# Negated row maxima as three rows of the stacked query operand, placed by a DMA for each batch, in a six-stage decoder kernel

## The reference

```python
q = (x @ wq + bq) / sqrt(8); k = c @ wk + bk; v = c @ wv + bv     # c is x, or the context (64, 77, 128)
attn = softmax(einsum('bhqd,bhkd->bhqk', q, k), axis=-1)
out = einsum('bhqk,bhkd->bhqd', attn, v)
x = layernorm(x + (out @ wo + bo))
```

## Time and profile before

| | us |
|---|---|
| Median of 3 runs | 5520.02 (5518.24 to 5530.13) |
| The profiled execution | 5516.31 |
| Its span in the trace | 5514.6 |
| First scores to the tail of F / N / Y in the trace | 3240 to 3750 / 4204 to 4755 / 4820 to 5258 |
| PE busy in the span | 4032.9 (73%) |
| DVE busy | 4394.4 (80%) |
| ACT busy | 2740.3 (50%) |
| POOL busy | 3137.7 (57%) |

### The profile page before, as it was taken

One profiled execution on the slowest core, in us unless ns is written; L12 is line 12 of the kernel. 1 busy time (PEld: TensorE's weight loads), 2 busy tenths in 40 slices (PEclk: granted clock), 3 DMA queues, 4 the chain that ended last, 5 costly groups with the idle time before them and its releaser, 6 DMA issues. The chain is left out here.

```text
span 5514.6 us, 104615 instructions
## 1 busy us (share of the span) xinstructions
PE 4032.9 (73%) x29692; PEld 2318.9 (42%) x29692; DVE 4394.4 (80%) x8517; ACT 2740.3 (50%) x6405; POOL 3137.7 (57%) x3426
## 2 busy tenths in 40 slices
PE   5777787777777877775788958885465888698843
PEld 2333233333323333232466636664464666466611
DVE  5999999999999999997688867764245777676678
ACT  3545554554555545553577724444564555344434
POOL 6877777777777777785677732324553222333302
PEclk8999899998998989988899969996786888799955
DMA  2111111111011101110566446654125555365511
GB/s 83 66 43 58 68 67 48 54 67 68 33 68 67 67 37 65 68 66 13 92 113 106 80 90 111 110 102 146 53 86 99 93 103 100 74 115 107 99 39 31
DMA packets 320201, 420.84 MB, mean 76 GB/s; under 512 B 40000, under 2 KB 301713, under 8 KB 309137
## 3 DMA queue, kind: packets, MB, share of 16 engines
q1 hardware_dynamic: 315536, 408.35, 31.9%
q0 software_dynamic: 4352, 8.95, 0.5%
HBM read 307.65 MB, written 109.58 MB: 76 GB/s over the span
## 5 line engine op out<-in xcount | busy, mean ns | idle before, releaser
L2199 POOL TENSOR_TENSOR m_h<-m_dtu,m_Bb 128x512 f32<-128x512 f32 x1024 | 1589.8, 1581 | 225.8 <-PE bank L1834 218.9
L1834 PE MATMUL bank<-m_h,ident 128*128 128x512 f32 x2048 | 1215.6, 684 | 497.3 <-DVE m_h L2098 484.3
L1834 PEld LDWEIGHTS bank<-m_h,ident 128*128 128x128 f32 x2048 | 361.6, 206 | 1162.5 <-DVE m_h L2098 1016.6
L2092 DVE TENSOR_TENSOR_SCAN m_h<-m_dA,m_h 128x512 f32<-128x512 f32 x512 | 755.2, 1475 | 6.3 <-DVE m_sz L2025 6.3
L2098 DVE TENSOR_TENSOR m_h<-m_h,bank 128x512 f32<-128x512 f32 x1024 | 672.3, 657 | 5.3 <-DVE m_h L2092 2.9
L2092 DVE TENSOR_TENSOR_SCAN m_h<-bank,m_h 128x512 f32<-128x512 f32 x512 | 620.5, 1212 | 28.1 <-DVE m_sz L2025 11.8
L1981 ACT ACTIVATE bank<-m_dt,m_A 128x512 f32<-128x512 f32 x512 | 352.4, 688 | 494.7 <-DVE m_h L2092 436.1
L1981 ACT ACTIVATE m_dA<-m_dt,m_A 128x512 f32<-128x512 f32 x512 | 367.2, 717 | 430.6 <-DVE m_h L2092 426.8
L688 DVE TENSOR_REDUCE x_nm<-bank 128x4 f32<-128x308 f32 x512 | 242.8, 474 | 182.3 <-PE bank L359 179.2
L531 ACT ACTIVATE x_sm<-bank,x_nm 128x77 f32<-128x77 f32 x1024 | 317.9, 335 | 59.9 <-DVE x_nm L688 59.4
L688 DVE TENSOR_REDUCE f_nm<-bank 128x4 f32<-128x512 f32 x256 | 175.8, 688 | 119.2 <-PE bank L359 118.6
(11 more groups left out here) (425 smaller groups left out, 10400.9 us busy)
## 6 DMA issues: line engine op xcount, KB each, us to landing
m_Bb<-m_B SPq DMA_DIRECT2D x32, 4096.0 KB, 12.1
x_Ks<-x_k_parts SPq DMA_DIRECT2D x32, 462.0 KB
x_q_parts<-x_qp SPq DMA_DIRECT2D x32, 384.0 KB, 4.1
x_Qs<-x_q_parts SPq DMA_DIRECT2D x32, 384.0 KB
f_Ks<-f_k_parts SPq DMA_DIRECT2D x16, 768.0 KB
a_Ks<-a_k_parts SPq DMA_DIRECT2D x16, 768.0 KB
x_xp<-x_stage SPq DMA_DIRECT2D x32, 256.0 KB
x_Qs<-x_q_parts SPq DMA_DIRECT2D x32, 256.0 KB
```

The costliest lines, as they stand in the source:

```text
L1834: pe.matmul(banks[4 + c], ident[:], h[:, k % RING, :], start=(s == 0), stop=(s == NS - 1)).then_inc(s_ya.sem, 1)
L2092: v.tensor_tensor_scan(h[:, k % RING, :], decays[k % AHEAD], h[:, k % RING, :], 0.0, ALU.mult, ALU.add).then_inc(s_h.sem, 1)
L2199: pool.tensor_tensor(h[:, k % RING, :], dtu[:, d, c, :], Bb[:, d, s, :], ALU.mult).then_inc(s_dB.sem, 1)
```

## The change

In stages without a gate the negated maxima no longer have matmuls of their own. They are three more rows of `Qs`, rows 96 to 98, against rows of ones in `Ks`. The scores are taken with these rows at zero, `shifted` with the maxima in them:

- ACT issues one DMA for each batch (`place_rows`), from `nmT` (48 rows x 128) to three rows x 16 heads x 128 of `Qs`, as soon as `nmT` is there. `sel`, its three selections on POOL and its matmuls are gone.
- `fill_stack` sets the three rows of a group back to zero by one more DMA, from rows 99 to 101.
- `shifted` and `exp` of a batch begin two slots later: chunk 0 in slot 3 of the next step, and chunks 1 to 3 in slots 0 to 2 of the step after that. `values` stays in its slots. The wait for `nmT` in `shifted` becomes a wait for the DMA.
- The stacks' rows are 0 to 23 and 64 to 87 (in stage X too). The 48 rows of `Ks` come in two DMAs of 24, and the memset of `Ks` in two, rows 0 to 95 and 96 to 127, the latter 1.0 without a gate and 0.0 with one.

```diff
-    PARTS, ROWS = 3, 6 * DH
+    PARTS = 3
     K_TIMES = (3, 2, 1)
+    Q_ROWS = (0, 8 * DH, 10 * DH)
+    K_ROWS = ((0, 0, 3), (8 * DH, 3, 6))
+    MAX_ROW = 96
+    FILLS = len(Q_ROWS) + len(K_ROWS) + (gate is None)
+    T_AT = 3
...
+        def turned_chunk(c):
+            return (1, c - T_AT) if c >= T_AT else (2, c - T_AT + 4)
+        def placed(i, lb):
+            return s_mr[lb % 2].sem, s_mr[lb % 2].at(4 * (i + lb // 8) + lb % 8 // 2 + 1)
...
-                at = 0
-                for parts in K_TIMES:
-                    fill(Qs[at * DH:(at + parts) * DH, par], dram_q[par, 0:parts])
-                    at += parts
-                fill(Ks[0:ROWS, par], dram_k[par])
+                for row, parts in zip(Q_ROWS, K_TIMES):
+                    fill(Qs[row:row + parts * DH, par], dram_q[par, 0:parts])
+                if gate is None:
+                    sp.dma_start(Qs[MAX_ROW:MAX_ROW + PARTS, par], Qs[MAX_ROW + PARTS:MAX_ROW + 2 * PARTS, par]).then_inc(s_stk[par].sem, 16)
+                for row, lo, hi in K_ROWS:
+                    fill(Ks[row:row + (hi - lo) * DH, par], dram_k[par, lo:hi])
...
-            def shifted(b, lb, c):
+            def shifted(b, lb, c, rows):
                 l, q = lb // GB, lb % GB
-                pe.wait_ge(s_nmT.sem, s_nmT.at(b + 1))
+                pe.wait_ge(*rows)
                 pe.wait_ge(s_e.sem, s_e.at(b, c + 1 - 2))
                 for h in range(4):
                     hh = 4 * c + h
                     o = bankT[c % 2][0:sk, h * S:(h + 1) * S]
-                    pe.matmul(o, Ks[:, l, hh, q * sk:(q + 1) * sk], Qs[:, l, hh, q * S:(q + 1) * S],
-                              start=True, stop=False)
-                    ins = pe.matmul(o, sel[:, hh, 0:sk], nmT[:, lb % 2, :], start=False, stop=True)
+                    ins = pe.matmul(o, Ks[:, l, hh, q * sk:(q + 1) * sk], Qs[:, l, hh, q * S:(q + 1) * S],
+                                    start=True, stop=True)
...
+            def place_rows(b, lm, rows):
+                act.wait_ge(s_nmT.sem, s_nmT.at(b + 1))
+                act.sem_inc(s_step, 1)
+                q = lm % GB
+                act.dma_start(Qs[MAX_ROW:MAX_ROW + PARTS, lm // GB, :, q * S:(q + 1) * S], nmT[0:PARTS * H, lm % 2, :]).then_inc(rows, 16)
...
-            dve.memset(Ks[:], 0.0).then_inc(s_zero.sem, 1)
-            if gate is None:
-                dve.memset(nmT[:], 0.0).then_inc(s_zero.sem, 1)
+            dve.memset(Ks[0:MAX_ROW], 0.0).then_inc(s_zero.sem, 1)
+            dve.memset(Ks[MAX_ROW:P], 1.0 if gate is None else 0.0).then_inc(s_zero.sem, 1)
```

More of the change, by code:

```diff
@@ L87, in attention @@
     TAIL = 6
-    ident, identb, ones_row, sel = const["ident"], const["identb"], const["ones_row"], const["sel"]
+    ident, identb = const["ident"], const["identb"]
     half_pow = const["half_pow"]
@@ L170, in attention @@
         s_mid = sem("mid_ready", 2); s_lo = sem("lo_ready", 2)
-        s_ps = sem("parts_stored", 16 * (PARTS + 1)); s_stk = [sem(f"stack_loaded{l}", 16 * (PARTS + 1)) for l in range(2)]
+        s_ps = sem("parts_stored", 16 * (PARTS + 1)); s_stk = [sem(f"stack_loaded{l}", 16 * FILLS) for l in range(2)]
         s_ln = sem("front_var", 1); s_lp = sem("front_pow", 1); s_xn = sem("front_norm", 1)
@@ L174, in attention @@
         s_S = sem("scores", 4); s_Sf = sem("scores_used", 4); s_nmp = sem("max_parts"); s_T = sem("max_transposed")
-        s_nmT = sem("max_rows"); s_st = sem("shifted", 4); s_e = sem("exp", 4)
+        s_nmT = sem("max_rows"); s_mr = [sem(f"max_rows_placed{p}", 16) for p in range(2)]; s_st = sem("shifted", 4); s_e = sem("exp", 4)
         s_gp = [sem(f"gate_loaded{l}", 16) for l in range(2)]; s_tw = sem("weights_turned", 4); s_ev = sem("weights_copied", 4)
@@ L187, in attention @@
         bankMb = bankM.bitcast(BF16)
-        NZ = 2 + (gate is None) + (sk < P)
+        NZ = 3 + (sk < P)
         NW = sum(1 for t in (bq, bk, bv, bo) if t is not None) + 4 + (2 if ln is not None else 0) + (2 if rms else 0)
@@ L431, in step @@
                         turn_weights(b - 1, (lb - 1) % 8, c)
[L432 to L435, removed]
+                else:
+                    k, chunk = turned_chunk(c)
+                    if live(k):
+                        shifted(b - k, (lb - k) % 8, chunk, placed(i, lb - k))
+                    if c == 0 and live(1):
                         turn_max(b - 1, (lb - 1) % 8)
-                elif live(1):
-                    shifted(b - 1, (lb - 1) % 8, c - 1)
                 if live(2):
@@ L546, in step @@
                 else:
[L547 to L550, removed]
+                    k, chunk = turned_chunk(c)
+                    if live(k):
+                        exp(b - k, (lb - k) % 8, chunk)
                 if c == 0 and live(4):
@@ L554, in step @@
                     act.activation(oT[:], bankY[:, 0:S], ACT.Copy).then_inc(s_oT.sem, 1)
+                if c == 0 and live(1) and gate is None:
+                    place_rows(b - 1, (lb - 1) % 8, placed(i, lb - 1)[0])
             def slots(i, lb, c, last):
@@ L699, in split_maxima, with maxima_rows @@
                 v.tensor_tensor(nmp[:, p, 2, :], nm[:, p, 1, :], nmp[:, p, 1, :], ALU.subtract).then_inc(s_nmp.sem, 1)
-            def maxima_rows(v, ch, b, lm):
+            def maxima_rows(v, ch, b, lm, rows):
                 v.wait_ge(s_T.sem, s_T.at(b + 1))
-                v.wait_ge(s_st.sem, s_st.at(b - 1))
+                v.wait_ge(*rows)
                 v.tensor_copy(nmT[0:PARTS * H, lm % 2, :], bankMb[0:PARTS * H, 0:S]).then_inc(s_nmT.sem, 1)
@@ L755, in step @@
                 if c == 0 and live(1) and gate is None:
-                    maxima_rows(v, ch, b - 1, (lb - 1) % 8)
+                    maxima_rows(v, ch, b - 1, (lb - 1) % 8, placed(i, lb - 3))
                 if gate is not None:
@@ L2628, in constants @@
     ones_row = st.enter_context(nc.sbuf_tensor("ones_row", [1, P], F32))
-    sel = st.enter_context(nc.sbuf_tensor("sel", [P, H, P], BF16))
     half_pow = st.enter_context(nc.sbuf_tensor("half_pow", [P, 4 * GB], F32))
@@ L2636, in _ @@
             pool.memset(identb[:], 0.0).then_inc(s, 1)
-            pool.memset(sel[:], 0.0).then_inc(s, 1)
             pool.memset(ones_row[:], 1.0).then_inc(s, 1)
             pool.memset(half_pow[:], -0.5).then_inc(s, 1)
-            pool.wait_ge(s, 5)
+            pool.wait_ge(s, 4)
             pool.affine_select(out=ident[:], in_=ident[:], compare_op=ALU.not_equal, fill=1.0, base=0,
@@ L2644, in _ @@
                                pattern=[[-1, P]], channel_multiplier=1).then_inc(s, 1)
[L2645 to L2650, removed]
+            pool.wait_ge(s, 6)
+    return {"ident": ident, "identb": identb, "ones_row": ones_row, "half_pow": half_pow}
 def build(nc, a, out, stages="MXFNYQ"):
```

## The result

The changed kernel takes 5779.4 us (median of 4 runs, 5775.3 to 5781.9) against 5519.4: a ratio of 1.047, 95% interval 1.0455 to 1.0485. It is slower, and 219 us above the top of the predicted range. Its profiled execution spans 5775.7 us, 261 more than before.

What follows compares the result with a forecast made beforehand. PE was nearest to full, F and Y mostly following it, N largely DVE; terms -115 + 15 + 19 + 4 + 25 - 8 + 10 + 1 + 6 = -43 gave 5477 us, forecast 5470, range 5385 to 5560.

Steps and rivals of the forecast that it cites:

- The new DMA: Placing the maxima in `Qs`: lands in 2.3 us, one 0.4 us stall a group, +19 us, bounds 0 and +130.
- In the long ones the slack is over 4 us: Time to spare for the placed rows in a group's long steps, against 1.9 to 2.2 us in its shortest.
- The matmuls removed: 1024 `sel` matmuls fewer on PE in each of F, N and Y: -115 us, bounds -50 and -165.
- The two slots: `shifted` two slots later leaves the exponential one slot ahead of `values`, sometimes late: +15 us, bounds 0 and +60.
- The fill: Stack loads, 17.6 us in F and 14.8 in Y: +4 us at four stage starts, +25 in mid-stage.
- A: Rival: everything hides, fill 12.2 us in F and never late, 5353 us, or 5400 with half; chance 0.22.
- B: Rival: the fill becomes the bound, 20 us in F, 17 in Y; 5574 at worst, some 5520; chance 0.15.
- Starts: Kernel start without `sel` setup -8 us; second memset +10 in N, +1 elsewhere; first and last steps +6.
- C: Rival: placed rows late in every step before `shifted` of chunk 0; slower, 5557 to 5717 us; chance 0.12.
- D: Rival: DVE takes over at once, -50 us in place of -115, 5505 to 5520 us; chance 0.11.
- 15 to 20% behind PE: DVE's busy time against PE's in stages F, N and Y, as read from the earlier profile.
- three steps less two slots of 1.3 and less 2.0: Time left for Y's mid-stage fill: 15 us before unevenness, about equal to the need of 14.8.

Runs made afterwards that it cites:

- e1: Changed kernel without the placement DMA, maxima left out of the exponent: 5392.5 us, ratio 0.975 to the kernel before.
- e2: Changed kernel with the stack filled only for the first two groups of each stage without a gate, placements kept: 5485.3 us, ratio 0.992.
- e10: Kernel before with only `shifted` and the exponential moved two slots later, one-hot matmuls and old rows kept: 5443.6 us, ratio 0.983.
- e11: Kernel before with only the new stack rows (0-23 and 64-87), five fills in place of four: 5513.5 us, ratio 0.997.
- e13: Kernel before without its one-hot matmuls (maxima left out of the exponent), old order kept: 5461.9 us, ratio 0.988.
- e16: Kernel before with the two-slot move and the new rows, one-hot matmuls kept, no placement DMA: 5399.1 us, ratio 0.977.

## Why the prediction was wrong, step by step

**The new DMA** is the step that failed. It said: "I take 2.3 us, from 1.6 to 5 when it shares the engines with a fill", and hence +19, bounds 0 and +130. The 2.3 was about right where no fill is under way (2.2 to 3.7 us where PE waited for it). The upper bound was the miss: beside a fill it took 11.1 to 14.5 us in F and N, 8.7 to 10.3 in Y. The term is +386 us (score sum of e1 to that of the changed kernel). I had taken the 5 us for a price of sharing bandwidth; it is a place in a line, so its bound was the fill's own length, and that stood in the earlier trace rows: 16.6 and 13.8. The earlier trace rows had the fill's issue (3503.12) 6 us ahead of the next turn of the maxima (3508.94), so that this placement had to fall inside the fill. The 391 us of waits are near the 386 in sum, but not by stage: 161, 115 and 115 of waits against 103, 124 and 159 of time. Of the 386, 290 go with the fills (e2); in the other 96 is the issue on ACT, for which I took SP's 0.33 us where it takes 0.74.

**"In the long ones the slack is over 4 us"** failed with it. The placement hit was that of the third step of a group, issued 4 us behind the fill. The short first step, which I watched, has none of more than 1 us in the groups that I read.

**The matmuls removed**: -115, bounds -50 and -165; measured -50 in the old order and -25 or -17 in the new. The sum priced PE's work where PE set the pace. In F it set it less than its 85% of busy time said, and PE's work there fell by 28 us less than the 62, at a lower clock.

**The two slots**: +15, bounds 0 and +60; measured -86. The sign is wrong. I asked who comes closer together (exponential and `values`: e10 has 9.8 us of such waits in N) and not who comes apart (`nmT` and `shifted`). By luck the two errors nearly cancel: matmuls, move and rows give -126, where my terms for matmuls and move gave -100.

**The fill**: +4 at the starts and +25 in mid-stage. The starts: 16.1, 15.0 and 13.7 us, where F and Y had 16.6 and 13.8. Neither A's 12.2 nor B's 20. New rows without the copy take 14.7 (e11). Mid-stage it was not late: e10 waits 5 us for `Ks` in all.

**Starts**: the kernel's first DMA is issued at 2.60 us in place of 10.61, -8 as predicted. In N the second memset holds back the sums of squares: 9 us from the first memset before, 24 now:

```profile
4243.69 6.88 DVE L609 MEMSET a_Ks<- 96x8192 uint32 x1 [10.67 <-issue]
4254.05 13.71 DVE L610 MEMSET a_Ks<- 32x16384 bf16 x1 [3.47 <-issue]
4267.79 1.92 DVE L652 TENSOR_REDUCE a_ms<-a_sq 128x64 f32<-128x512 f32 x2
```

From the first memset to the fill's issue it is 40.4 us in place of 28.2, so 12.2 where I had 10.

**The rivals.** C had the right place (`shifted` behind the placement) and side, with 0.12, but not the mechanism: it wanted 3.5 to 5 us in every step. What happened is one stall of 6 to 11 us in each group, and of up to 13 at the first. D, DVE taking over, was in part true of F.

**Slips.** DVE is not 15 to 20% behind PE in all three stages: by the earlier trace rows it is 17, 10 and 22%. In Y three steps less two slots of 1.3 and less 2.0 leave 15.8 us, not 15. Neither bears on the outcome.

## What to carry to other kernels

Ask of a small DMA on the path what large transfer will be under way when it is issued, and bound its landing by what is left of that one, not by its own size; put it ahead of the large one in time, and cut the large one around it. Before pricing removed work by an engine's busy share, look for short waits in both directions between two engines: here moving one consumer a slot later gave more than all the work it was moved to save. Run the parts of a change apart: the good part of this one was the by-product.

## What the runs showed of the hardware

- A DMA of 12 KB on ACT's queue lands 2.2 to 3.7 us after the start of its issue when no fill is under way, and about with the end of the fill when one was issued up to 4 us earlier on SP's queue: 7.6, 13.6, 22.6 us for three lengths. None of its packets moved for the first 9.9 us of the 13.6.
- Issuing it takes 0.74 us on ACT and 0.73 on SP (medians); the fill's large DMAs take 0.33 each on SP.
- The same 1536 KB onto the stack's rows took 25.9 us in DMAs of 8 rows, 16.1 in DMAs of 8 to 24, to the first scores.
- A memset of bf16 ones took 13.71 us for 16384 elements a row, on 32 partitions, and one of zeros 6.88 for 8192 of 32 bits on 96: the same 0.84 ns an element.
- With 1024 matmuls fewer in a stage, the granted clock of F fell from 0.92 to 0.85, in the old order (e13) and behind the move (e16 to e1). In Y it fell from 0.96 to 0.91 in the old order, and only from 0.99 to 0.98 behind the move.
